# One row of the attention score by way of DRAM instead of two transposes, and a new order of work, in a four-layer graph network on one core

## The chip, the cores and the metric

The kernel runs on one core of a Trainium2 chip. The metric is the time of one execution on the device, in microseconds (us); smaller is better. The core's engines are named as the profile names them: PE (TensorE), DVE (VectorE), ACT (ScalarE), POOL (GpSimd) and SP (SyncE, which here only issues DMAs). Each runs its own instructions strictly in the order in which they are written, and waits on semaphores that the others raise.

## What is computed

32 graphs of 256 nodes with 256 features go through four layers. Each adds its output to its input and normalises over the features:

```python
x = _layernorm(x + _L0_gnn_ref(x, adj, W, b))      # ((adj @ (x @ W + b)) / row sums of adj
x = _layernorm(x + _L1_gnn_ref(x, adj, kernel))    # relu((adj @ x) @ kernel), masked
x = _layernorm(x + _L2_gnn_ref(x, adj, kernel, b)) # relu(D (adj + I) D x kernel + b)
x = _layernorm(x + _L3_gnn_ref(x, adj, Wv, bv, aw, ab, Wk, bk))
```

The last layer is the one that the change touches:

```python
sj = Xw @ aw[:d, 0]                      # Xw = X @ Wv + bv
si = Xw @ aw[d:, 0]
e = leaky_relu(sj[:, None, :] + si[:, :, None] + ab[0], negative_slope=0.2)
alpha_matrix = A * jnp.exp(e)
transition = alpha_matrix / (jnp.sum(alpha_matrix, axis=-1, keepdims=True) + 1e-12)
for k in range(3):
    H = H + Xk @ Wk[k] + bk[k]
    Xk = jnp.einsum('bij,bjd->bid', transition, Xk)
return relu(H)
```

So each graph needs its score once as a column (one number for each node, on the partitions) and once as a row of 256 numbers that every partition holds.

## The kernel before

The graphs are worked on four at a time: slot g = 0 to 3, group k = 0 to 7. A product is split into three fp32r parts (lo x hi, hi x lo, hi x hi) over two halves of the contraction and two output halves, which makes 12 matmuls. `product` (lines 262 to 264) and `product_by_turns` (line 272) write them. The "hi" part is a rounded copy, made on ACT (line 564), and the "lo" part is the rest, made on DVE or POOL.

The steps on PE are named s1 to s11, each for a slot and a group:

- s1: x W0; s2: adj times that, with the row sums in an extra column. Both are layer 0.
- s3, s4: layer 1. s5, s6: layer 2.
- s7: four transposes of x3, the input of layer 3 (line 341), so that `fea` holds it by features.
- s8a: x3 times Wk[0] and the two attention vectors. DVE adds the bias (`p0`, line 1261) into the tile P0, of which columns F and F+1 are the two scores of each node.
- s8b: x3 times Wk[1] and Wk[2], 512 columns wide, into the one PSUM tile `pair[1]`. ACT (`p12`) and DVE (`p2_lo`, line 1226) empty it.
- s9: two transposes of column F+1 of P0, broadcast over 128 columns (line 365). They leave the row of scores on all partitions in `ring[g]`.
- s10, s11: alpha times what came of s8b, and alpha times that (`q`, `q_hi`, `q_lo` between them).

After s9, ACT adds the column to the row (`logits`, line 624), DVE applies the leaky part (`leaky`), ACT takes exp (line 630), POOL multiplies by adj (`alpha`, line 959), and ACT and DVE split the result into `alpha_hi` and `alpha_lo`.

Each layer's normalisation runs DVE `statistics` (line 1206) and `variance_eps` (1211, 1212), POOL `power` and `mean_scale` (929, 946) and ACT `norm` (645). `norm(2, g, k)` writes X3, which also holds the output of layer 3, so it waits until the store of the group before (`x3_free`) is through.

The order of work on each engine is written out by hand in `first_iteration`, in `iteration(k)`, which a loop runs six times, and in `last_iterations`, which holds groups 6 and 7. Work of three groups is mixed in each: layers 2 and 3 of group k, layers 0 to 2 of group k+1, and s1 of group k+2. SP issues nearly all loads and stores in a fixed order of its own. Ahead of s1, PE runs 20 transposes on the identity matrix (`warm_up`, line 388).

Of the kernel before, what the change touches and what calls it, by code (L numbers as in the profile page):

```python
# [35 lines left out]
def build(nc, x, xT, adjT, w0, w1, w2, wk, wvT, aw, bv, ab, b0, b2, bk, out):  # L36
# [7 lines left out]
    with ExitStack() as ctx:  # L44
# [72 lines left out]
        y_ready = [sem4(f"y{l}_ready") for l in range(4)]  # L117
# [15 lines left out]
        P12_ready, Q_ready = sem("P12_ready"), sem("Q_ready")  # L133
        s_ready, e_ready, ex_ready, al_ready = sem("s_ready"), sem("e_ready"), sem("ex_ready"), sem("al_ready")
# [14 lines left out]
        def h_bank(g, first=False):  # L149
            return ring[g][:, :] if first else pair[g // 2][:, g % 2, :]  # L150

# [33 lines left out]
        def _(sp):  # L185
# [23 lines left out]
            def store(g, k):  # L209
                sp.wait_ge(x_ready[3][g], k + 1)  # L210
                sp.dma_start(graph(out, g, k), X3[g][:, :]).then_inc(x3_free[g], 16)

            def iteration(k, left):
# [13 lines left out]
                for g in range(SLOTS):  # L227
                    store(g, k)
# [26 lines left out]
        def _(pe):  # L255
# [68 lines left out]
            def s5(g, kn, first=False):  # L324
                pe.wait_ge(xd_lo_ready, count(g, kn))
                pe.wait_ge(diag_ready[g], kn + 1)
                if not first:
                    pe.wait_ge(y_ready[3][g], kn)
# [8 lines left out]
            def s7(g, k):  # L337
                pe.wait_ge(x_ready[2][g], k + 1)
                for f in range(2):
                    for t in range(2):  # L340
                        last = nc.tensor.transpose(ring[g][:, f * N + t * P:f * N + (t + 1) * P],  # L341
                                                   nodes(X3[g])[:, t, f * P:(f + 1) * P], ident[:, :])
                last.then_inc(s7_done[g], 1)
# [58 lines left out]
            def first_iteration():  # L402
                s1(0, 0, first=True)
                s2(0, 0, first=True)
                s1(1, 0, first=True)
                s1(2, 0, first=True)
                s1(3, 0, first=True)
                s2(1, 0, first=True)
                s2(2, 0, first=True)
                s2(3, 0, first=True)  # L410
                s1(0, 1, first=True)
                s3(0, 0, first=True)
                s3(1, 0, first=True)
                attention_vectors()
                s4(0, 0)
                s4(1, 0)
                s3(2, 0, first=True)
                s3(3, 0, first=True)
                s4(2, 0)
# [1320 lines left out]
```

## Time and profile before

| | |
|---|---|
| median of 3 runs | 560.35 us (559.84 to 560.39) |
| the profiled execution, its own time | 560.77 us |
| its span in the profile | 559.0 us |
| PE, busy | 536.1 us, 96% |
| DVE, busy | 499.7 us, 89% |
| POOL, busy | 459.1 us, 82% |
| ACT, busy | 418.5 us, 75% |
| data moved by DMA | 44.73 MB, mean 80 GB/s |

The span is what the profile covers, and the 1.8 us between it and the time of the same execution lie outside. Matmuls are pipelined: a matmul's own duration is longer than the distance between the starts of two, and the distance is what it costs.

### The profile page before, as it was taken

The page shows a single profiled execution, that of the slowest core. Times are in us where ns is not written, and L with a number is a line of the kernel's source. Part 1 is how long each engine was busy: PE and PEld are TensorE (multiplying, and loading weights), DVE is VectorE, ACT ScalarE, POOL GpSimd, SP SyncE. Part 2 cuts the span into 40 slices and gives each one's busy share as a digit, 9 for nine tenths or more (in the row PEclk, how much of TensorE's full clock was granted, in tenths as well). Part 3 has the DMA queues.
Part 4 walks back from the last instruction along what each step waited for, and adds up shares of the span by engine and source line. Part 5 has one row for each costly group of instructions (what it writes and reads, how often), then busy time and mean ns, then how long its engine had stood idle before and what let it go on. Part 6 is the DMA issues. An engine that isn't in the chain of part 4 may idle for free.

```text
span 559.0 us, 12279 instructions
## 1 busy us (share of the span) xinstructions
PE 536.1 (96%) x4064; PEld 511.6 (92%) x4064; DVE 499.7 (89%) x1221; ACT 418.5 (75%) x929; POOL 459.1 (82%) x575
## 2 busy tenths in 40 slices
PE   6799999999999999999999999999999999999983
PEld 6799999999999999999999999999999998998873
DVE  3999989989999889989899899998899898899676
ACT  4468787687876878687876978768796777875763
POOL 4688898989988899888989899888998898573253
PEclk9899999999999999999999999999999999999998
DMA  8824011340032301422114401324013300201001
GB/s 282 288 65 123 27 39 57 115 169 11 26 121 86 131 19 38 130 102 87 38 35 133 162 9 35 113 88 137 19 38 119 103 24 1 77 2 57 19 1 75
DMA packets 25222, 44.73 MB, mean 80 GB/s; under 512 B 3184, under 2 KB 3824, under 8 KB 25200
## 3 DMA queue, kind: packets, MB, share of 16 engines
q1 hardware_dynamic: 24336, 43.79, 24.3%
q10 hardware_dynamic: 864, 0.66, 0.4%
q8 instruction: 12, 0.20, 0.1%
q14 instruction: 10, 0.08, 0.0%
HBM read 36.05 MB, written 8.39 MB: 79 GB/s over the span
## 4 chain that ended last, share of the span: by engine, by line
PE 82%; DVE 10%; DMA 2%; issue 2%; ACT 2%; SPq 1%; POOL 0%; ACTq 0%; POOLq 0%; DVEq 0%
PE pair L272 37%; PE ring L262 12%; PE ring L264 12%; PE ring L263 12%; PE ring L341 3%; PE pair L262 2%; PE pair L264 2%; PE pair L263 2%; DVE stats L1206 2%; DMA xT_in<-xT_dram 1%; PE ring L365 1%; DVE ring L1286 1%; DVE nod_lo L1244 1%; DMA out_dram<-X 1%; DVE X L1235 1%
## 5 line engine op out<-in xcount | busy, mean ns | idle before, releaser
L645 ACT ACTIVATE X<-X,nmr,rstd 128x256 f32<-128x256 f32 x192 | 104.3, 596 | 51.6 <-POOL nmr L946 49.8
L929 POOL TENSOR_TENSOR rstd<-powin,minus_half 128x2 f32<-128x2 f32 (+1 forms) x124 | 104.1, 842 | 34.9 <-DVE nmean L1212 34.9
L1206 DVE BATCH_NORM_STATS2 stats<-X 128x6 f32<-128x512 f32 x128 | 89.9, 708 | 1.2
L262 PE MATMUL ring<-adj_hi,nod_lo 128*128 128x256 f32 x256 | 73.3, 286 | 1.3 <-DVE nod_lo L1244 1.3
L262 PE MATMUL ring<-W_hi,fea_lo 128*128 128x256 f32 x256 | 72.6, 284 | 1.0 <-DVE fea_lo L1198 1.0
L264 PE MATMUL ring<-adj_hi,nod_hi 128*128 128x256 f32 x256 | 72.3, 282 | 0.0
L263 PE MATMUL ring<-adj_lo,nod_hi 128*128 128x256 f32 x256 | 72.2, 282 | 0.0
L264 PE MATMUL ring<-W_hi,fea_hi 128*128 128x256 f32 x256 | 71.7, 280 | 0.0
L263 PE MATMUL ring<-W_lo,fea_hi 128*128 128x256 f32 x256 | 71.4, 279 | 0.0
L564 ACT ACTIVATE fea_hi<-ring 128x512 fp32r<-128x512 f32 x96 | 56.8, 593 | 18.4 <-PE ring L264 12.4
L1198 DVE TENSOR_TENSOR fea_lo<-ring,fea_hi 128x512 fp32r<-128x512 f32 x96 | 63.8, 683 | 6.5 <-ACT fea_hi L564 6.4
L959 POOL TENSOR_TENSOR tmp<-tmp,adj_in 128x512 f32<-128x512 f32 x32 | 46.7, 1467 | 23.4 <-ACT tmp L630 23.4
L262 PEld LDWEIGHTS ring<-adj_hi,nod_lo 128*128 128x128 f32 x256 | 48.7, 190 | 2.6 <-DVE nod_lo L1244 2.0
L262 PEld LDWEIGHTS ring<-W_hi,fea_lo 128*128 128x128 f32 x256 | 48.1, 188 | 1.7 <-issue 0.9
L263 PEld LDWEIGHTS ring<-adj_lo,nod_hi 128*128 128x128 f32 x256 | 48.8, 191 | 0.3
L264 PEld LDWEIGHTS ring<-adj_hi,nod_hi 128*128 128x128 f32 x256 | 48.8, 191 | 0.0
L263 PEld LDWEIGHTS ring<-W_lo,fea_hi 128*128 128x128 f32 x256 | 48.2, 188 | 0.0
L264 PEld LDWEIGHTS ring<-W_hi,fea_hi 128*128 128x128 f32 x256 | 48.1, 188 | 0.0
L917 POOL TENSOR_TENSOR adj_lo<-adj_in,adj_hi 128x512 fp32r<-128x512 f32 x32 | 41.0, 1299 | 8.3 <-ACT adj_hi L564 8.0
L967 POOL TENSOR_TENSOR h_lo<-P,h_hi 128x512 fp32r<-128x512 f32 x32 | 39.8, 1245 | 9.3 <-ACT h_hi L564 9.3
L952 POOL TENSOR_SCALAR X<-X,nmean,rstd 128x256 f32<-128x256 f32 x64 | 41.8, 662 | 1.1 <-POOL rstd L933 0.7
L272 PE MATMUL pair<-WB_hi,fea_lo 128*128 128x512 f32 x128 | 41.8, 407 | 0.2 <-DVE h_lo L1226 0.2
(123 smaller groups left out, 1910.0 us busy)
## 6 DMA issues: line engine op xcount, KB each, us to landing
adj_in<-adjT_dram SPq DMA_DIRECT2D x64, 256.0 KB, 2.8
xT_in<-xT_dram SPq DMA_DIRECT2D x32, 256.0 KB, 3.3
X<-x_dram SPq DMA_DIRECT2D x32, 256.0 KB, 2.6
out_dram<-X SPq DMA_DIRECT2D x32, 256.0 KB, 2.0
P<-wk_dram SPq DMA_DIRECT2D x3, 256.0 KB, 3.9
P<-w_dram SPq DMA_DIRECT2D x2, 256.0 KB, 5.9
X<-bk_dram SPq DMA_DIRECT2D x3, 128.0 KB, 4.2
P<-w_dram ACTq DMA_DIRECT2D x1, 256.0 KB, 3.8
```

What stands on the lines that cost most here:

```text
L262: mm(o, lhs(1, t, i), rhs(0, t), start=t == 0, stop=False)
L263: mm(o, lhs(0, t, i), rhs(1, t), start=False, stop=False)
L264: last = mm(o, lhs(0, t, i), rhs(0, t), start=False, stop=t == 1)
L272: last = mm(o, lhs(left, t, i), rhs(right, t), start=t == 0 and left == 1, stop=t == 1 and left == right)
L564: return nc.scalar.activation(dst, src, ACT.Copy)
L645: last = nc.scalar.activation(nodes(X[min(l + 1, 3)][g])[:, t, :], nodes(X[l][g])[:, t, :], ACT.Identity, scale=rstd[l][g][:, t:t + 1], bi ...
L917: tt(adj_lo[g][:, :], adj_in[g][:, :], adj_hi[g][:, :], ALU.subtract).then_inc(adj_ready, 1)
L929: tt(rstd[l][g][:, 0:n], powin[l][g][:, 0:n], minus_half[:, 0:n], ALU.pow).then_inc(rstd_ready[l], 1)
L952: last = ts(nodes(X1[g])[:, t, :], nodes(X0[g])[:, t, :], nmean[0][g][:, t:t + 1], rstd[0][g][:, t:t + 1], ALU.add, ALU.mult)
L959: tt(tmp[g][:, :], tmp[g][:, :], adj3_in[g][:, :], ALU.mult).then_inc(al_ready, 1)
L1198: tt(fea_lo[g][:, :], ring[g][:, :], fea_hi[g][:, :], ALU.subtract).then_inc(ready, 1)
L1206: nc.vector.bn_stats(stats[l][g][:, :], by_turns(X[l][g])).then_inc(st_ready[l], 1)
```

## The change

For groups 0 to 6, s9 goes. In its place SP waits for P0, stores its column F+1 to a small DRAM tensor (256 numbers, each 4 bytes), waits until that has landed, and loads it back as a row that is broadcast to all 128 partitions, into the second half of `tmp[g]`. `logits` waits for that load and reads `tmp` in place of the PSUM tile. Group 7 keeps s9.

With that, some waits change: s3 of the next group waits for `x3T_ready` and no longer for `s_ready`; s10 of an even slot waits for `p2_lo` of its own slot and not for that of slot 3; layers 2 and 3 count their `y_ready` on one semaphore each.

At the start, the loads of X0 come later (the first two slots' xT and adj first), and the loads of the attention vectors are issued by ACT only after the first h_hi parts. In group 7, x3 stands in X0 and not in X3, so `norm(2, g, 7)` doesn't wait for a store, and the last normalisation, that of slot 3, is done on DVE (`norm3`), with neither POOL's `mean_scale` nor ACT's `norm`. Finally the order of work is written anew on all engines, in all three parts.

```diff
+            def row_of_x3(g, k):
+                sp.wait_ge(P0_ready, count(g, k))
+                with nc.allow_non_contiguous_dma(reason="one number of each node"):
+                    sp.dma_start(row[g].rearrange("t p -> p t"), mixed(P0[g])[:, :, F + 1]).then_inc(row_out, 16)
+                sp.wait_ge(row_out, 16 * count(g, k))
+                sp.dma_start(nodes(tmp[g])[:, 1, :], row[g:g + 1].rearrange("a t p -> a (t p)").to_broadcast([P, N])).then_inc(row_in[g], 16)
...
-                if left >= 2:
+                if left >= 1:
+                    row_of_x3(0, k)
                     for g in range(SLOTS):
-                        load_x(g, k + 2)
-                if left >= 1:
+                        if g < SLOTS - 1:
+                            row_of_x3(g + 1, k)
+                        if left >= 2:
+                            load_x(g, k + 2)
                     for g in range(SLOTS):
                         load_adj3(g, k + 1)
...
             for g in range(SLOTS):
-                for load in (load_xT, load_adj, load_x):
+                for load in (load_xT, load_adj):
                     load(g, 0, before=False)
+                if g >= 1:
+                    load_x(g - 1, 0, before=False)
+            load_x(SLOTS - 1, 0, before=False)
...
             def s3(g, kn, first=False):
                 pe.wait_ge(x1_lo_ready, count(g, kn))
                 if not first:
-                    pe.wait_ge(s_ready, count(g, kn - 1))
+                    pe.wait_ge(x3T_ready, count(g, kn - 1))
...
                 pe.wait_ge(al_lo_ready, count(g, k))
-                pe.wait_ge(P2_ready, count(SLOTS - 1, k))
+                pe.wait_ge(P2_ready, count(SLOTS - 1 if g % 2 else g, k))
...
             def first_iteration():
                 s1(0, 0, first=True)
+                s1(1, 0, first=True)
                 s2(0, 0, first=True)
-                s1(1, 0, first=True)
+                s2(1, 0, first=True)
                 s1(2, 0, first=True)
                 s1(3, 0, first=True)
-                s2(1, 0, first=True)
                 s2(2, 0, first=True)
                 s2(3, 0, first=True)
-                s1(0, 1, first=True)
                 s3(0, 0, first=True)
...
-                s9(0, k)
+                s3(0, k + 1)
+                s7(2, k)
                 s8a(1, k)
-                s7(2, k)
-                s3(0, k + 1)
                 s8b(1, k)
+                s7(3, k)
                 s8a(2, k)
                 s4(0, k + 1)
-                s9(1, k)
-                s9(2, k)
-                s7(3, k)
+                s8a(3, k)
                 s8b(2, k)
...
-            def logits(g, k):
-                act.wait_ge(s9_done, count(g, k))
+            def logits(g, k, last=False):
+                if last:
+                    act.wait_ge(s9_done, g + 1)
+                else:
+                    act.wait_ge(row_in[g], 16 * k + 16)
+                summand = ring[g][:, 0:N] if last else nodes(tmp[g])[:, 1, :]
...
-            def norm(l, g, k):
+            def norm(l, g, k, last=False):
                 act.wait_ge(nmr_ready[l], count(g, k))
-                if l == 2:
+                if l == 2 and not last:
                     act.wait_ge(x3_free[g], 16 * k + 16)
...
+            def norm3(g, k):
+                dve.wait_ge(rstd_ready[3], count(g, k))
+                for t in range(2):
+                    half = X0[g][:, t * F:(t + 1) * F]
+                    last = ts(half, half, nmean[3][g][:, t:t + 1], rstd[3][g][:, t:t + 1], ALU.add, ALU.mult)
+                last.then_inc(x_ready[3][g], 1)
```

How the change moves instructions is seen at three places.

The first is SP, inside its loop, behind the four loads of xT. Before, the four loads of X0 and the loads of adj for layer 3 follow:

```order
L192 DMA xT_in<-xT_dram 128x512
L197 DMA X_0<-x_dram 128x512
L197 DMA X_1<-x_dram 128x512
L197 DMA X_2<-x_dram 128x512
L197 DMA X_3<-x_dram 128x512
```

Now (register instructions of the waits stand between):

```order
L216 DMA row_dram<-P_1 128x2x1
L217 REGISTER_ALU
L218 DMA tmp<-row_dram 128x256
L201 DMA X_0<-x_dram 128x512
L214 REGISTER_ALU
L216 DMA row_dram<-P_2 128x2x1
L217 REGISTER_ALU
L218 DMA tmp<-row_dram 128x256
L201 DMA X_1<-x_dram 128x512
```

Each row is a store and a load, and SP waits for the first before it issues the second; the loads of X0 stand between the rows.

The second is DVE at the start, from the first xT_lo on. L1295 is `first_xT_lo`, L1202 `h_lo_part`, L1217 and L1218 `sums0`, L1308 `first_x_bias`, L1302 `first_y0`. Before:

```order
L1295 TENSOR_TENSOR xT_lo0<-xT_in0,xT_hi0 128x512
L1202 TENSOR_TENSOR h_lo0<-ring0,h_hi0 128x2x256
L1295 TENSOR_TENSOR xT_lo1<-xT_in1,xT_hi1 128x512
L1295 TENSOR_TENSOR xT_lo2<-xT_in2,xT_hi2 128x512
L1295 TENSOR_TENSOR xT_lo3<-xT_in3,xT_hi3 128x512
L1217 TENSOR_SCALAR powin0_0<-pair0 128x2
L1218 RECIPROCAL rinv0<-pair0 128x2
L1202 TENSOR_TENSOR h_lo1<-ring1,h_hi1 128x2x256
L1202 TENSOR_TENSOR h_lo2<-ring2,h_hi2 128x2x256
L1202 TENSOR_TENSOR h_lo3<-ring3,h_hi3 128x2x256
L1308 TENSOR_TENSOR X0_0<-X0_0,b0_bc 128x512
```

Now, where L1323, L1336, L1217, L1237, L1238 and L1330 are the same functions:

```order
L1323 TENSOR_TENSOR xT_lo1<-xT_in1,xT_hi1 128x512
L1336 TENSOR_TENSOR X0_0<-X0_0,b0_bc 128x512
L1217 TENSOR_TENSOR h_lo0<-ring0,h_hi0 128x2x256
L1323 TENSOR_TENSOR xT_lo2<-xT_in2,xT_hi2 128x512
L1217 TENSOR_TENSOR h_lo1<-ring1,h_hi1 128x2x256
L1237 TENSOR_SCALAR powin0_0<-pair0 128x2
L1238 RECIPROCAL rinv0<-pair0 128x2
L1330 SCALAR_TENSOR_TENSOR X0_0<-pair0,rinv0,X0_0 128x256 x2
L1224 BN_STATS stats0_0<-X0_0 128x6
```

The part for slot 3's xT and the h_lo parts of slots 2 and 3 have moved behind `first_y0` of slot 0.

The third is the end of DVE's program. Before, it closes with slot 3's variance and mean:

```order
L1286 SCALAR_TENSOR_TENSOR ring3<-ring3,rinv3,P0_3 128x256 x2
L1211 TENSOR_SCALAR powin3_2<-stats3_2 128x2
L1212 TENSOR_SCALAR nmean3_2<-stats3_2 128x2
L1291 SCALAR_TENSOR_TENSOR X3_3<-ring3,X3_3 128x512
L1206 BN_STATS stats3_3<-X3_3 128x6
L1211 TENSOR_SCALAR powin3_3<-stats3_3 128x2
L1212 TENSOR_SCALAR nmean3_3<-stats3_3 128x2
```

Now:

```order
L1312 SCALAR_TENSOR_TENSOR X0_3<-ring3,X0_3 128x512
L1224 BN_STATS stats3_3<-X0_3 128x6
L1231 TENSOR_SCALAR powin3_3<-stats3_3 128x2
L1232 TENSOR_SCALAR nmean3_3<-stats3_3 128x2
L1318 TENSOR_SCALAR X0_3<-X0_3,nmean3_3,rstd3_3 128x256 x2
```

The order of the rest is as it was; two instructions of 128x256 have been added behind it.

## Rows read from the trace of the kernel before

**Rows 1.** The page: an engine's busy time, and the clock in 40 slices.

```profile
PE 536.1 (96%) x4064; PEld 511.6 (92%) x4064; DVE 499.7 (89%) x1221; ACT 418.5 (75%) x929; POOL 459.1 (82%) x575
PEclk9899999999999999999999999999999999999998
```

**Rows 2.** Busy time by stretch: stretch, its length, each engine's busy us, PEclk, DMA.

```profile
123.83:189.27 65.44, 65.44 (x507) 63.04 (x506) 60.83 (x149) 51.70 (x116) 59.00 (x73) 1.00 0.25 80
```

**Rows 3.** What PE waited for in the whole span: us in total, times, longest.

```profile
PE pair L272 <- DVE X L1302: 3.1, 1, 3.1
PE pair L272 <- issue: 1.7, 1, 1.7
PE pair L272 <- DVE h_lo L1202: 1.4, 1, 1.4
PE ring L262 <- DVE nod_lo L1244: 1.3, 2, 0.9
PE ring L341 <- ACT X L645: 1.0, 1, 1.0
```

**Rows 4.** Timeline of PE around an s7 and an s9: start, us, instruction.

```profile
462.19 0.60 PE L341 MATMUL ring<-ident,X 128*128 128x128 f32 x4
462.63 0.38 PE L365 MATMUL ring<-ident,P 128*128 128x128 f32 x2
462.76 0.48 PE L272 MATMUL pair<-WA_hi,fea_lo 128*128 128x258 f32 x2
463.09 0.40 PE L272 MATMUL pair<-WA_lo,fea_hi 128*128 128x258 f32 x2
```

**Rows 5.** Timeline of PE at the start: the first matmul of s1(0), and two successive ones.

```profile
6.62 0.36 PE L262 MATMUL ring<-W_hi,xT_lo 128*128 128x256 f32 x1 [1.34 <-DVE xT_lo L1295]
...
11.87 0.28 PE L264 MATMUL ring<-W_hi,xT_hi 128*128 128x256 f32 x1
11.99 0.28 PE L262 MATMUL ring<-W_hi,xT_lo 128*128 128x256 f32 x1
```

**Rows 6.** The chain that ended last, 0 to 60 us: start, us, what.

```profile
5.12 8.17 DMA xT_in<-xT_dram
...
19.96 0.88 DVE X L1302 x2
...
30.56 0.79 PE pair L396 x8
...
49.60 0.39 PE ring L262
```

**Rows 7.** Busy time by stretch, after the long wait at the start.

```profile
21.00:23.00 2.00, 2.00 (x11) 2.00 (x12) 1.82 (x8) 0.00 (x0) 0.81 (x2) 0.60 1.04 260
```

**Rows 8.** DMA issues, KB each, us to landing: 0 to 40 us.

```profile
ab_bc<-ab_dram ACTq DMA_DIRECT2D x1, 0.5 KB, 6.6
```

**Rows 9.** The same, in the whole span.

```profile
adj_in<-adjT_dram SPq DMA_DIRECT2D x64, 256.0 KB, 2.8
out_dram<-X SPq DMA_DIRECT2D x32, 256.0 KB, 2.0
```

**Rows 10.** Timeline of ACT in a group of the loop: start, us, instruction.

```profile
210.56 0.60 ACT L564 ACTIVATE fea_hi<-ring 128x512 fp32r<-128x512 f32 x1
211.04 0.85 ACT L624 ACTIVATE tmp<-ring,P 128x256 f32<-128x256 f32 x2
```

**Rows 11.** The chain that ended last: an s8b of group 0.

```profile
66.71 2.81 PE pair L272 x12
```

**Rows 12.** The chain that ended last, 500 to 559 us.

```profile
512.43 4.09 DMA out_dram<-X
...
516.61 1.10 ACT X L645 x2
...
554.36 0.70 POOL rstd L929
...
555.36 0.60 ACT X L645
```

More of the change, by code:

```diff
@@ L731, in iteration @@
                 from_ring(2, s7_done, k, fea_hi, x3T_hi_ready)
-                xT_hi_part(1, k + 2)
                 from_ring(0, s3_done, k + 1, fea_hi, t1_hi_ready)
                 norm(2, 3, k)
+                logits(0, k)
+                from_ring(3, s7_done, k, fea_hi, x3T_hi_ready)
+                xT_hi_part(3, k + 2)
+                x1_hi(1, k + 1)
+                p12(1, k)
+                x1_sum(1, k + 1)
+                x1_hi(2, k + 1)
+                logits(1, k)
+                exp(0, k)
@@ new lines, in iteration @@
+                p12(2, k)
+                exp(1, k)
+                diag_hi(0, k + 1)
+                x1_hi(3, k + 1)
+                from_ring(1, s3_done, k + 1, fea_hi, t1_hi_ready)
+                alpha_hi_part(0, k)
+                logits(2, k)
+                logits(3, k)
+                from_ring(2, s3_done, k + 1, fea_hi, t1_hi_ready)
+                exp(2, k)
+                exp(3, k)
+                p12(3, k)
+                alpha_hi_part(1, k)
+                x1_sum(2, k + 1)
@@ new lines, in last_iterations @@
+            def last_iterations(k):
+                h_hi_part(0, k + 1)
+                adj_hi_part(0, k + 1)
+                h_hi_part(1, k + 1)
+                h_hi_part(2, k + 1)
+                h_hi_part(3, k + 1)
+                adj_hi_part(1, k + 1)
+                adj_hi_part(2, k + 1)
+                adj_hi_part(3, k + 1)
+                z0(0, k + 1)
+                z0(1, k + 1)
+                norm(2, 0, k)
+                norm(2, 1, k)
+                from_ring(0, s7_done, k, fea_hi, x3T_hi_ready)
+                z0(2, k + 1)
+                z0(3, k + 1)
+                from_ring(1, s7_done, k, fea_hi, x3T_hi_ready)
+                norm(2, 2, k)
+                p12(0, k)
+                x1_hi(0, k + 1)
+                from_ring(2, s7_done, k, fea_hi, x3T_hi_ready)
+                norm(2, 3, k)
+                logits(0, k)
@@ new lines, in last_iterations @@
+                norm(2, 0, k + 1, last=True)
+                from_ring(2, s5_done, k + 1, fea_hi, t2_hi_ready)
+                from_ring(0, s7_done, k + 1, fea_hi, x3T_hi_ready)
+                from_ring(3, s5_done, k + 1, fea_hi, t2_hi_ready)
+                norm(2, 1, k + 1, last=True)
+                from_ring(1, s7_done, k + 1, fea_hi, x3T_hi_ready)
+                norm(2, 2, k + 1, last=True)
+                p12(0, k + 1)
+                logits(0, k + 1, last=True)
+                from_ring(2, s7_done, k + 1, fea_hi, x3T_hi_ready)
@@ L867, in last_iterations @@
+                norm(2, 3, k + 1, last=True)
+                p12(1, k + 1)
+                logits(1, k + 1, last=True)
+                from_ring(3, s7_done, k + 1, fea_hi, x3T_hi_ready)
+                norm(3, 0, k)
                 exp(0, k + 1)
-                p12(1, k + 1)
-                norm(2, 3, k + 1)
-                logits(1, k + 1)
-                from_ring(3, s7_done, k + 1, fea_hi, x3T_hi_ready)
+                exp(1, k + 1)
                 p12(2, k + 1)
-                exp(1, k + 1)
@@ L1390, in first_iteration @@
                 xd_lo(1, 0)
-                weights_lo()
                 xd_lo(2, 0)
```

961 lines of the change are left out of this document (457 added, 504 removed).

## Prediction

> **What bounds the kernel now.** I read the page first: PE is busy 96% of the span, and its clock is at the full 2.4 GHz but for the second and the last of 40 slices [rows 1]. Then the stretches: one turn of the loop (group 1's, the others differ by some hundredths) takes 65.44 us, and PE is busy for 65.44 of them, while DVE has 60.83, POOL 59.00 and ACT 51.70 [rows 2]. So the loop, six turns and 393 us of the span, is PE's own work without a hole, and what leaves PE there leaves the time. Then the waits: all that PE waits for in the whole span lies outside the loop [rows 3], the longest 3.1 and 1.4 us at the start and 1.7 and 1.0 us in the last two groups. Last, the chain to the first 60 us, and the chain of the end [rows 6, 12].
>
> **What s9 costs.** One place shows it: s7's four transposes start at 462.19, s9's two at 462.63, the next matmul pair at 462.76, and that pair then takes 0.33 us to the next where pairs otherwise follow in 0.24 [rows 4]. s7 takes 0.44 and leaves the same 0.09 behind it when it stands alone; together they cost 0.57 + 0.09 = 0.66, of which I give s9 a third, 0.22 us. The change takes 28 of the 32 away: 28 x 0.22 = **6.1 us**, 0.88 in each turn of the loop. The bounds: 28 x 0.13 = 3.6 us if the slower pair behind is not saved, 6.2 at most.
>
> **What comes in its place.** Two DMAs a graph, on SP's queue, which PE never waits for. Neither has its like in the trace. The store is 256 numbers of 4 bytes; nearest are the 256 KB store of the output, 2.0 us, and the 4-byte broadcast of ab in the crowded start, 6.6 us [rows 8, 9]. The load is 1 KB into each partition; nearest are the 256 KB loads, 2.8 us, and again 6.6 [rows 9, 8]. A quarter of the DMA engines' time is taken in the loop [rows 2], so I take values near the uncrowded rows: 2.8 for the store, 2.5 for the load, and with two issues of about 0.45 on SP some 6.2 us for a row.
>
> The Trainium skill (DMA: Bandwidth & Descriptors, rules for kernel authors, and the anatomy of one DMA) says that a strided last dimension becomes one descriptor for each element, and that a DMA has about 2 us that don't depend on its size, most of it the receipt of the write. By that, two dependent DMAs are an estimated 4 us before any descriptor; the trace's 2.0 us for an output store agrees with the second rule, and no row here shows the first.
>
> Is there room for 6.2 us? I lay the new order of PE on a line, with s6(0) at 0, 1.43 us for a product of twelve 256-column matmuls (steps of 0.12 [rows 5]), 0.44 for s7, 2.81 for s8b [rows 11]. s8a(0) ends at 13.8, and s10(0), the first to need alpha, comes at 36.0 (before, at 39.7). Slot 0's row is back at about 21, and ACT reaches `logits(0)` at 20 and has nothing urgent until s7(3) ends at 23.2. Slots 2 and 3 are closer: P0(2) is ready at about 26, SP issues its store, waits, issues the load, a load of X0, then slot 3's store, waits again: 26 + 2 x (0.45 + 2.8) + 3 x 0.45 - 0.45 + 2.5, about 36. ACT wants it at 35 to 36, by steps of about 0.5 us per instruction [rows 10]. What is queued behind `logits(3)` on ACT is from_ring(2), exp(2), exp(3), p12(3) and alpha_hi(1); PE's s10(1), at 41.8, needs the last, split on DVE. With slot 3's row at 36 alpha_hi(1) is through at about 40.7 and DVE, in its own order, comes to the split just ahead of 42; until the row is some 0.8 us later still, it costs PE nothing. Slot 2's q must pass DVE, ACT and POOL by s11(2) at 51.8, and I find it there at 52.0. So nothing is far late, and some of it has no slack: DVE's 60.8 us now stand in a turn of 64.57, 94%, and POOL's 59.0, 91%. I charge **1.0 us** for small holes over all turns; between 0 (as now) and 5 us (0.7 a turn, nearly all of what s9 gave).
>
> **The start.** s1(0) begins at 6.62 us [rows 5]; s5(2) begins at 49.60 [rows 6], and with it and s5(3), 2.9 us, s6(0) begins at 52.5. Between lie 24 products and the attention vectors' 12 small matmuls (8 of them in 0.79 [rows 6], so 1.2), 24 x 1.43 + 1.2 = 35.5 us of work in 45.9 us, so 10.4 are lost. Why: DVE holds its part of xT_in[3] (landed at 13.3, after 8.17 us) ahead of `first_y0(0)` at 19.96, which frees the PSUM pair for s2(2) [rows 6]; PE waits 3.1 us for it [rows 3], and then runs at a granted clock of 0.60 [rows 7], between 1.2 and 2.4 GHz: 11 matmuls in 2.00 us, 0.18 each for 0.12, so about 1.5 us more over the 24 of two s2.
>
> Now s1(1) fills the 1.4 us hole ahead of s2(0) (its xT is one load earlier). Then h_hi(1) on ACT waits behind xT_hi(2), which lands at about 10.1 by my estimate (the tenth load lands at 13.3, at 0.8 us a load, and it is now the sixth): s2(1) starts at 12.1, a hole of 0.9. `first_y0(0)` is through at 13.2, seven us earlier, so s2(2) and s2(3) wait only for their h_lo parts on DVE, about 0.7 each. s3(0) waits about 2.0 for x1_lo(0), which stands behind x_bias and y0 of slots 2 and 3. Behind it the products follow one another until s5(0), which waits 1.1 for xd_lo(0), behind `weights_lo` (some seven full-tile steps, about 4 us if a half tile takes 0.44 [rows 6] and a full one 0.6). These holes are my count along the new order, 5.4 us in all, with 0.4 for the slower first matmuls behind them: s6(0) at about 6.6 + 35.5 + 5.8 = 47.9. That is **4.5 us** less. Bounds: a gain of only 1.5 us if the 2 us hole also brings the low clock and DVE has another as long; of 8 us if the holes close.
>
> **The end.** From 500 us on PE idles in the waits of [rows 3]. The 1.0 us for ACT is `norm(2, 1)`, which waits for the store of the group before, 4.09 us in the chain [rows 12]; with x3 in X0 that wait is gone. The other holes there are at most 1.3, some of them for nod_lo on DVE [rows 3]. The 1.7 us ahead of s10(0) is p12(3) and p2_lo(3) after the last s8b; s10(0) no longer waits for them, but s10(1) does, 0.5 us after it could start. Counting on from there, DVE gets q(0) done at +3.3 and not +5.1 us, s11(0) starts at +5.4 and not +7.1, and then DVE's own chain of q, z3, y3 and statistics, which is full in both, brings most of it back: the last mean is 0.7 us earlier. `norm3` then costs two DVE instructions of 128x256 where POOL's product, two hand-overs and ACT's two instructions took from 554.36 + 0.70 = 555.06 to 555.36 + 1.10 = 556.46 [rows 12]. Such instructions on DVE take 0.44 each in other rows (first_y0's two, 0.88 [rows 6]); 0.9 for 1.4 saves 0.5. Sum: 1.0 + 0.5 (of the 1.3) + 0.7 + 0.5 = **2.7 us**. Bounds 0 (the holes move) and 5 (all close).
>
> **Sum.** 560.77 (the profiled execution's own time) - 6.1 - 4.5 - 2.7 + 1.0 = 548.5 us. That execution lay 0.42 above the median of the runs, so 548.1 us on the median's scale, 2.2% under it.
>
> **The rivals.**
>
> First, *the rows come late, and it ends slower than before*. The place is `logits(2)` and `logits(3)` on ACT, behind which stand exp, p12 and alpha_hi. My count has slot 3's row at 36 and 0.8 us of slack behind it. If each DMA takes X, it is back at 27.8 + 3 X, since SP waits for slot 2's store first. It decides where seven groups lose 13.3 us, 1.9 each: 27.8 + 3 X = 36.7 + 1.9, X = 3.6 us. At X = 4 a group loses 3.1, and the kernel takes 560.35 + 21.7 - 13.3 = 569 us; at 6.6, ab's in the crowd, far over 600. For it speaks that every element is a piece of its own; against it that the loop's DMA is mostly idle, and that uncrowded transfers a thousand times larger land in 2.0 to 2.8. Chance 0.08; about 569.
>
> Second, *another engine sets the turn*. DVE's 60.8 and its hand-overs don't shrink, and with PE's order tighter the turn stays near 65.3. Then the start, the end and 7 x 0.15 us count: 560.35 - 4.5 - 2.7 - 1.1 = 552 us. For it: 94% on DVE, and two places where I found needs and supplies within 0.3 us. Against it: in the trace before, equally close orders left PE no hole in 65.44 us. Chance 0.16.
>
> Third, *the start gives nothing*: holes of 2 us bring the granted clock of 0.60, as one of 3.1 us did while two of 1.4 didn't. Then 1.5 us in place of 4.5: 551 us. Chance 0.10, and the range holds it.
>
> Fourth, *all holes close* at start, end and in the loop: 560.35 - 6.1 - 8 - 4 = 542 us. Chance 0.06.
>
> **Chances and range.** The forecast has 0.60. The range, 543.5 to 555, holds the forecast, the second and the third, and leaves out the first and most of the fourth and of a wider second. Differences under 0.2% (1.1 us) can't be told from none in this kernel. Faster by more than that: all but the first rival and a piece of the second, 0.91; within 0.2%, 0.02; slower, 0.07.
>
> **What would show it.** In the profile after, PE has 56 fewer transposes, and its busy time is about 6 us less. The turn of the loop is about 64.6 us with PE busy throughout; if it is 65.4, the second rival is right, and the engine that PE waits for says where. If ACT's `tmp` of `logits` waits long for a DMA of `row_dram`, it is the first. s6(0) starts at about 48 us; the granted clock at 15 to 30 us tells the third. In the chain of the end, DVE's `norm3` takes under 1 us. I am wrong if a row takes much over 6 us to return, if the holes at the start don't shrink, or if PE's own work has grown at a place that I took as moved only.

## The result, and the profile after

The changed kernel takes 763.23 us (median of 4 runs, 760.77 to 766.86) against 560.37 us of the kernel before in the same job (4 runs, 559.84 to 561.73). The ratio is 1.361, interval 1.358 to 1.365: **slower by 203 us**. The forecast was 548.1 us. The profiled execution took 760.91 us, with a span of 759.1.

The page of the changed kernel: busy time of each engine, the granted clock, the shares of the chain that ended last, and one DMA row (size, median us to landing):

```profile
PE 580.8 (77%) x4008; PEld 540.8 (71%) x4008; DVE 518.7 (68%) x1223; ACT 415.3 (55%) x927; POOL 444.8 (59%) x574
...
PEclk9999877998779987799887997879988799779999
...
DMA 40%; DVE 37%; PE 11%; issue 6%; ACT 3%; SPq 2%; POOL 1%; ACTq 0%; DVEq 0%; POOLq 0%
...
row_dram<-P SPq DMA_DIRECT2D x28, 1.0 KB, 9.6
```

PE had 96% [rows 1] and has 77%. Its busy time has grown by 45 us although 56 transposes are gone, and the granted clock falls from 2.4 to 1.2 GHz twice in each turn. In the second turn it is 0.50 from 176.4 to 183.2 us and from 200.3 to 217.4, the second time with PE idle since 196.7 us; each matmul takes longer in these stretches. In the kernel before it fell once, at the start [rows 7]. The chain that ended last is a DMA's for 40% of the span. The last row is the price that the forecast had at 2.8 us: the row's store lands after 9.6 us.

The waits of the changed kernel over the span (engine and line, what it waited for, us in total, times, longest):

```profile
POOL tmp L975 <- ACT tmp L642: 200.9, 18, 18.5
ACT tmp L637 <- DMA tmp<-row_dram: 198.3, 27, 12.1
DVE tmp L1285 <- ACT tmp L637: 137.9, 21, 10.7
...
PE ring L279 <- DVE fea_lo L1213: 76.6, 7, 13.7
```

L637 is `logits`, L1285 the leaky part, L975 `alpha`: the wait for the row is handed down through ACT, DVE and POOL. PE's longest wait isn't for alpha. It is for `fea_lo` of layer 1, a step with no need of the row. It stands on DVE behind the leaky part, and its `fea_hi` on ACT behind `logits`, and those need the row.

SP's queue in the second turn (start, us, line, transfer; L216 is the row's store, L218 its load back, L201 a load of X0), from the store of slot 1's row on:

```profile
171.70 0.37 SPq L216 DMA_DIRECT2D row_dram<-P  x1
181.15 0.32 SPq L218 DMA_DIRECT2D tmp<-row_dram  x1
181.58 0.37 SPq L201 DMA_DIRECT2D X<-x_dram  x1
182.06 0.37 SPq L216 DMA_DIRECT2D row_dram<-P  x1
```

And the chain through it, with the first store of the next turn:

```profile
163.21 8.03 DMA row_dram<-P
171.70 9.44 DMA row_dram<-P
182.06 10.42 DMA row_dram<-P
193.44 9.51 DMA row_dram<-P
202.96 4.91 DMA tmp<-row_dram
258.26 8.04 DMA row_dram<-P
```

Four stores stand end to end, since SP waits for each to land before it issues anything else: 8.03 + 9.44 + 10.42 + 9.51 = 37.4 us, then a load of 4.9, and 2.3 for what SP issues between them, 44.7 us from P0(0) to the last row. A turn is 258.26 - 163.21 = 95.05 us, against 65.44 [rows 2].

### The profile page after: what moved, and what is told of

Same layout as the page of the kernel before. It is cut to its first block, busy times and chain, and to the rows that moved or that the text cites. A ratio compares the mean times of both kernels' runs of the same rounds, so it can differ in the third digit from the quotient of the medians.

```text
span 759.1 us, 12235 instructions
## 1 busy us (share of the span) xinstructions
PE 580.8 (77%) x4008; PEld 540.8 (71%) x4008; DVE 518.7 (68%) x1223; ACT 415.3 (55%) x927; POOL 444.8 (59%) x574
## 4 chain that ended last, share of the span: by engine, by line
DMA 40%; DVE 37%; PE 11%; issue 6%; ACT 3%; SPq 2%; POOL 1%; ACTq 0%; DVEq 0%; POOLq 0%
DMA row_dram<-P 33%; DVE stats L1224 6%; PE pair L289 6%; DMA tmp<-row_dram 5%; DVE nod_lo L1264 4%; DVE ring L1306 3%; DVE ring L1272 3%; DVE P L1298 3%; DVE powin L1231 3%; DVE h_lo L1217 2%; DVE X L1312 2%; DVE nmean L1232 2%; DVE X L1255 2%; PE ring L279 1%; DVE X L1277 1%
## 5 line engine op out<-in xcount | busy, mean ns | idle before, releaser
L975 POOL TENSOR_TENSOR tmp<-tmp,adj_in 128x512 f32<-128x512 f32 x32 | 41.6, 1305 | 201.4 <-ACT tmp L642 200.9
L279 PE MATMUL ring<-W_hi,fea_lo 128*128 128x256 f32 x256 | 75.9, 297 | 76.6 <-DVE fea_lo L1213 76.6
L637 ACT ACTIVATE tmp<-tmp,P 128x256 f32<-128x256 f32 x56 | 25.4, 501 | 198.3 <-DMA tmp<-row_dram 198.3
L945 POOL TENSOR_TENSOR rstd<-powin,minus_half 128x2 f32<-128x2 f32 (+1 forms) x124 | 99.8, 806 | 57.3 <-DVE nmean L1232 57.2
L1285 DVE SCALAR_TENSOR_TENSOR tmp<-tmp 128x512 f32<-128x512 f32 x32 | 22.0, 689 | 138.0 <-ACT tmp L637 137.9
L281 PE MATMUL ring<-W_hi,fea_hi 128*128 128x256 f32 x256 | 75.0, 293 | 0.0
L289 PE MATMUL pair<-WB_hi,fea_lo 128*128 128x512 f32 x128 | 45.9, 442 | 15.0 <-DVE h_lo L1246 15.0
L289 PE MATMUL pair<-WA_hi,fea_lo 128*128 128x258 f32 x128 | 31.4, 330 | 33.5 <-DVE P L1281 33.5
L280 PEld LDWEIGHTS ring<-W_lo,fea_hi 128*128 128x128 f32 x256 | 51.6, 202 | 0.0
L281 PEld LDWEIGHTS ring<-W_hi,fea_hi 128*128 128x128 f32 x256 | 51.5, 201 | 0.0
```

What stands on the lines that cost most here:

```text
L279: mm(o, lhs(1, t, i), rhs(0, t), start=t == 0, stop=False)
L280: mm(o, lhs(0, t, i), rhs(1, t), start=False, stop=False)
L281: last = mm(o, lhs(0, t, i), rhs(0, t), start=False, stop=t == 1)
L289: last = mm(o, lhs(left, t, i), rhs(right, t), start=t == 0 and left == 1, stop=t == 1 and left == right)
L945: tt(rstd[l][g][:, 0:n], powin[l][g][:, 0:n], minus_half[:, 0:n], ALU.pow).then_inc(rstd_ready[l], 1)
L975: tt(tmp[g][:, :], tmp[g][:, :], adj3_in[g][:, :], ALU.mult).then_inc(al_ready, 1)
```

## The experiments

Three theories stood behind them. **A**: the rows' latency, in series on SP, is the loss. **B**: the new order is. **C**: leaving s9 out never gave 6 us, since another chain sets the turn. Later ones are named where they come in. Each kernel was timed beside the kernel before.

### Without the rows, and the rows alone

```diff
-                    row_of_x3(0, k)
-                            row_of_x3(g + 1, k)
...
-                    act.wait_ge(row_in[g], 16 * k + 16)
-                summand = ring[g][:, 0:N] if last else nodes(tmp[g])[:, 1, :]
+                    act.wait_ge(P0_ready, count(g, k))
+                summand = ring[g][:, 0:N] if last else bk_bc[:, 0:N]
```

> The changed kernel with both DMAs of the row left out in groups 0 to 6: logits adds the bias tile bk_bc in place of the row, so the output is not the reference's. Theory A (the two DMAs of a row, 9.6 and 4.6 us to landing and issued one after another by SP, make all the loss): the turn of the loop falls from 95.3 to about 65 us, PE is busy all through it, and the time is 548 to 553 us (the start gained 1.3 us and not 4.5). Theory B (the new order and the new waits lose by themselves): the turn stays well over 66 us and the time is over 565 us.

577.17 us against 561.27, ratio 1.0275 (1.0217 to 1.0332). So 186 of the 203 us are the rows, and some 16 us are the new order's own. Theory A missed its 548 to 553 us, and what theory B named did happen (a turn of 68.67 us, over 565 us in all): both are right in part, and A has by far the larger part. The second kernel is the kernel before with nothing but the rows in place of s9:

> The kernel before, with the row by DRAM in groups 0 to 6 in place of the transposes, and nothing else of the change but the two waits that it needs. Theory A: SP's chain of four rows, some 45 us, is the loss in any order; the turn is 90 to 105 us and the time 720 to 800 us, much like the changed kernel. Theory B: the old order keeps most of its time, under 650 us.

```diff
+                    row_of_x3(0, k)
...
-                s9(0, k)
...
-                act.wait_ge(s9_done, count(g, k))
+                    act.wait_ge(row_in[g], 16 * k + 16)
```

825.22 us, ratio 1.471 (1.466 to 1.476), over the 800 that theory A had at most. The rows alone cost 264 us in the old order, and not by SP's series alone. In the chain of its second turn stand three rows, each with its load (8.65 + 4.87, 8.69 + 4.40 and 8.74 + 4.95 us), and between them steps of ACT, DVE and PE: P0 of the next slot is made behind work that waits for the row of another. The new order bears the rows better and still isn't made for them.

In the kernel without rows the room that a row has can be read. DVE's P0 of the four slots in one turn:

```profile
206.07 0.69 DVE L1278 TENSOR_TENSOR P<-pair,bk_bc 128x516 f32<-128x516 f32 x1
212.88 0.69 DVE L1278 TENSOR_TENSOR P<-pair,bk_bc 128x516 f32<-128x516 f32 x1
215.69 0.69 DVE L1278 TENSOR_TENSOR P<-pair,bk_bc 128x516 f32<-128x516 f32 x1
220.79 0.68 DVE L1278 TENSOR_TENSOR P<-pair,bk_bc 128x516 f32<-128x516 f32 x1
```

And ACT's logits of the same slots, the last row with slots 2 and 3 (slot 3's half of it from 225.5 on):

```profile
211.90 0.91 ACT L634 ACTIVATE tmp<-bk_bc,P 128x256 f32<-128x256 f32 x2
219.03 0.90 ACT L634 ACTIVATE tmp<-bk_bc,P 128x256 f32<-128x256 f32 x2
...
224.67 1.71 ACT L634 ACTIVATE tmp<-bk_bc,P 128x256 f32<-128x256 f32 x4
```

From the end of P0 to the logits there are 5.1, 5.5, 8.3 and 4.0 us, and 18.8 from the first P0 to the last logits. The changed kernel needs 44.7 for the same stretch: 25.9 us more. Its turn is 95.05 - 68.67 = 26.4 us longer than this kernel's. The rows' loss is that stretch, once for each of the seven groups (7 x 26.4 = 185 us).

### What sets the store's price

The kernel before, with four small stores more in each turn whose landing nothing waits for but their own next issue; slot 0's has the changed kernel's form:

```diff
+                    sp.dma_start(dst, src).then_inc(side_done[g], 16)
...
+            forms = [(side["fa"].rearrange("t p -> p t"), b2_bc[:, :].rearrange("p (t f) -> p t f", t=2)[:, :, 5]),
+                     (side["fb"], b2_bc[:, 0:2]),
+                     (side["fc"], b2_bc[:, 0:1]),
+                     (side["fd"][:, :, 0].rearrange("t p -> p t"), b2_bc[:, :].rearrange("p (t f) -> p t f", t=2)[:, :, 5])]
```

fa is 256 numbers of 4 bytes side by side in DRAM, as the row is; fb 128 pieces of 8 bytes side by side; fc 128 numbers of 4 bytes side by side; fd 256 numbers of 4 bytes, one every 64 bytes.

> The kernel before, with four small stores more in each turn of the loop that nothing waits for: 256 numbers of 4 bytes side by side in DRAM (as the row's), 128 pieces of 8 bytes, 128 pieces of 4 bytes, and 256 of 4 bytes that lie 64 bytes apart. Theory C (the price goes by the number of pieces): 8 to 10 us for both forms of 256, 4.5 to 6 for both of 128. Theory D (it goes by pieces that meet in the same lines of DRAM): side by side 8 to 10, 64 bytes apart 3 to 4; 128 of 8 bytes about 5 to 8. The kernel's own time stays within 1 us of before in both.

```profile
fa_dram<-b_bc SPq DMA_DIRECT2D x6, 1.0 KB, 9.8
fb_dram<-b_bc SPq DMA_DIRECT2D x6, 1.0 KB, 8.3
fc_dram<-b_bc SPq DMA_DIRECT2D x6, 0.5 KB, 10.2
fd_dram<-b_bc SPq DMA_DIRECT2D x6, 1.0 KB, 5.9
```

These are the page's DMA rows: count, size, median us to landing. The time is 561.63 us (one run), so the stores cost the kernel nothing where nobody waits. Half as many pieces (fc) cost as much as all (fa): it isn't their number. But the four rows can't be compared as they stand. fb is issued while fa is still landing, and fd while fc is:

```profile
X<-x_dram SPq DMA_DIRECT2D x1, 256.0 KB, 7.5
...
211.50:214.00 2.50, 2.50 (x12) 2.01 (x12) 2.50 (x7) 2.50 (x7) 2.50 (x4) 1.00 0.00 0
```

The first line is a load of X0 that SP issued at 210.96 us, just before fb (211.40) and 6 us behind fa (204.99, landed at 214.69). In the kernel before such a load takes 2.5 us. The second has the columns of [rows 2]: for 2.5 us no DMA engine does anything, though the load and fb are both waiting. At the same place of the next kernel, where the store ahead is 1 KB in one piece, the load takes 2.6 us and the engines are busy for 0.43 of the stretch. So a store of pieces side by side holds back what is issued behind it until it has landed. fb waited 3.0 to 3.7 us for fa in this way, and fd 3.0 to 3.4 for fc. Without that wait an estimate is 5.0 us for fb and 2.8 for fd (medians of six).

A second kernel took four other forms:

> The same, with four other stores: 1 KB from one partition in one piece, 128 pieces of 64 bytes, 256 of 4 bytes with a node's two numbers side by side (as neighbours 4 bytes apart), and 256 of 4 bytes that lie 512 bytes apart. Theory C: about 2.5, 4.5 to 6, 8 to 10 and 8 to 10 us. Theory D: about 2.5, 2.5 to 4, 8 to 10, and 3 to 4 us.

```profile
fh_dram<-b_bc SPq DMA_DIRECT2D x6, 8.0 KB, 2.4
...
fi_dram<-b_bc SPq DMA_DIRECT2D x6, 1.0 KB, 5.7
```

fh is 128 pieces of 64 bytes, fi 256 numbers 512 bytes apart. Eight times the bytes land in 2.4 us. fi stands behind fg, whose form is side by side, and the load of X0 issued just ahead of fi takes 6.0 to 6.9 us, so fi's 5.7 hold such a wait as well. Theory D fits all of this: numbers of 4 bytes side by side make 10 us, 8-byte pieces side by side some 5, and numbers 64 bytes apart hardly more than whole 64-byte pieces. It isn't shown that a line of 64 bytes is the limit, since nothing between 8 and 64 bytes of distance was tried. The landing of the 1 KB store from one partition (ff) and of fg isn't shown by the profile.

### The changed kernel with a quick store

```diff
-                    sp.dma_start(row[g].rearrange("t p -> p t"), mixed(P0[g])[:, :, F + 1]).then_inc(row_out, 16)
+                    sp.dma_start(row[:, :], b2_bc[:, 0:16]).then_inc(row_out, 16)
...
-                sp.dma_start(nodes(tmp[g])[:, 1, :], row[g:g + 1].rearrange("a t p -> a (t p)").to_broadcast([P, N])).then_inc(row_in[g], 16)
+                sp.dma_start(nodes(tmp[g])[:, 1, :], b2.to_broadcast([P, N])).then_inc(row_in[g], 16)
```

> The changed kernel with both DMAs of a row in their places, but with other data: the store writes 64 bytes from each of 128 partitions (2.4 us in a run of mine) in place of 256 numbers of 4 bytes (7.9 to 10.4 us), the load spreads 1 KB of b2 to the partitions as before (4.6 us). The logits' row is then b2 and not the graph's own. A row takes about 2.4 + 4.6 + 1.0 = 8 us in place of 15. Theory A (the landing of the scattered store is what costs, through SP's wait, four times in a turn): between 7 and 28 us a turn come back of the 26.6 that the rows cost: turn 69 to 77 us, time 577 to 635 us. Rival (two dependent DMAs on SP cost it whatever the store's form, by taking the queue from the other loads): turn over 85, time over 700 us.

580.92 us, ratio 1.035 (1.033 to 1.038).

```profile
tmp<-b_dram SPq DMA_DIRECT2D x28, 128.0 KB, 3.1
...
row_dram<-b_bc SPq DMA_DIRECT2D x28, 8.0 KB, 1.4
```

Both DMAs, both waits and the order of SP's queue are as in the changed kernel, and of the rows' 32% over the kernel without them all but 0.8%, some 4 us, is gone. A row takes 1.4 + 3.1 us, about 4.5 (the landing is counted from the issue), within the 4 to 8 us that there are. This is what shows A: with the same DMAs, waits and order, the rows cost some 4 us at 4.5 us a row and 186 at 9.6 + 4.6. It doesn't tell the store from the load, since both are quicker here.

### One latency a row, and none in SP's series

```diff
-                sp.wait_ge(row_out, 16 * count(g, k))
-                sp.dma_start(nodes(tmp[g])[:, 1, :], ...).then_inc(row_in[g], 16)
```

The store itself now signals `row_in`.

> The changed kernel with the row's store alone: SP doesn't wait for it, there is no load, and ACT's logits wait for the store to land and add the bias tile (the logits' row isn't the graph's own; the load's work is left out). So each row costs one latency of 8 to 10.4 us, and none waits behind another's. Without rows, logits(g) comes 5.1, 5.5, 8.3 and 4.0 us behind its P0, so the stores are 2 to 6 us late. Theory A (latency, in series on SP): turn 69 to 75 us, time 580 to 620 us, against 763 with both DMAs in series. Rival J (the store's latency alone is the loss, the series and the load matter little): over 700 us.

653.9 us, ratio 1.167 (1.159 to 1.174): between the two expectations, and neither had the reason. The chain of this kernel in its second turn:

```profile
155.35 9.74 DMA row_dram<-P
...
165.12 0.92 ACT tmp L635 x2
...
166.06 0.69 DVE tmp L1283
166.75 0.62 DVE P L1279
...
167.39 13.00 DMA row_dram<-P
```

SP doesn't put these two stores in series; DVE does. P0(3), which the last store waits for, stands on DVE behind the leaky part of slot 1, which waits for that slot's store. So two latencies (here 9.7 and 13.0) stand end to end in each turn whatever SP does. The 13.0 is longer than a store alone; it was issued 4.8 us behind slot 2's. That was in the order of the instructions, and I hadn't looked for it: a late row delays the next one's making.

### What s9's absence is worth

The kernel before without s9 in groups 0 to 6, no rows, nothing moved:

```diff
-                s9(0, k)
...
-                s9(3, k)
...
-                act.wait_ge(s9_done, count(g, k))
+                    act.wait_ge(P0_ready, count(g, k))
```

> The kernel before, with s9 left out in groups 0 to 6 and no row in its place: logits adds the bias tile, so the output is not the reference's; s3 waits for x3T_ready. All else, the order too, is as before. If the term of 6.1 us is right, the turn of the loop is 64.6 us and the time 554 to 555. It also tells theory A from theory B for the run without rows (577 us, turn 68.7): if the old order keeps PE full at 64.6, then the new order of the loop itself costs 4.1 us a turn; if the old order's turn also stays at 65.4 or more, something that comes with the missing s9 does.

560.32 us against 559.96, ratio 1.0003 (0.9988 to 1.0018): nothing. The stretch of one turn, columns as in [rows 2]:

```profile
189.20:254.60 65.40, 65.16 (x498) 62.43 (x497) 60.03 (x149) 51.52 (x116) 59.17 (x73) 1.00 0.25 78
```

PE's own 65.44 have become at most 65.16, and the turn is 65.4 to 65.5 as before. Along the turn PE is 0.69 us early at s4(1) (36.18 us behind s6(0), where the kernel before has 36.87), 0.46 at s10(0), and no longer early at s4(3) (48.36 in both). The holes are short: s10(0) starts 1.72 us behind s4(2), where the kernel before has 1.40, and s4(3) 1.66 behind s11(0) for 1.42. s4(3) needs `fea_lo` of slot 3, which DVE makes behind the attention steps. So one product was put ahead of it:

```diff
-                s4(3, k + 1)
                 s1(0, k + 2)
+                s4(3, k + 1)
```

> The kernel before without s9 in the loop (the summand of the logits is the bias tile; work left out), as in the run before it of that kind, and with one product's place changed: s1(0, k+2) stands ahead of s4(3, k+1) on PE and not behind it. In the run without s9 PE was 0.69 us early at s4(1) and no longer early at s4(3): s4(3) waits for fea_lo of slot 3, at the end of a chain through DVE. Theory C (a chain of other engines, hidden under PE, has the same 65.5 us turn): the hole ahead of s4(3) closes, since PE has s1(0) to do there, but the chain itself isn't shorter, so that the turn stays at 65.2 to 65.6 us, or grows if s4(3) is now late by a whole product; time 558 to 561 us. Rival F (only the one place in PE's order eats the gain): the turn goes to 64.7 to 65.0, time 555 to 557 us.

561.54 us, ratio 1.0014 (0.9998 to 1.003). The long step of the chain that opens a turn, of two turns:

```profile
126.76 5.99 PE pair L272 x48
192.23 5.99 PE pair L272 x48
```

The turn is 65.47, and the rival, that one place in PE's order ate the gain, falls. C's forecast holds. Its reason, a chain over the other engines that is as long as PE's work was, and hidden since PE never waited for it, fits the holes, but no run shortened that chain, and which steps make it is open.

### Why the new order is slow without the rows

Without the rows the turn is 68.67 us, columns as above:

```profile
198.43:267.10 68.67, 66.35 (x497) 62.42 (x497) 63.47 (x149) 51.57 (x117) 58.25 (x73) 1.00 0.23 76
```

DVE has grown from 60.83 to 63.47 us with the same 149 instructions. Four kinds of step that read only SBUF are longer: the two `nod_lo` and the small ones of variance and mean (0.28 for 0.19 us). Two others with both sources in SBUF are shorter: the leaky part takes 0.68 us for 1.05, and `alpha_lo` 0.68 for 0.82. The statistics (L1221, 0.71) and those that read PSUM (`fea_lo`, 0.68) are unchanged. DVE at one place of it:

```profile
252.65 2.70 DVE L1261 SCALAR_TENSOR_TENSOR nod_lo<-X,rstd,nod_hi 128x256 fp32r<-128x256 f32 x4
```

and POOL beside it (L926 is `x_bias`, the addition of b0 to X0):

```profile
253.53 1.54 POOL L926 TENSOR_TENSOR X<-X,b_bc 128x512 f32<-128x512 f32 x1
```

Four such steps take 1.66 us where POOL does something else. The test cuts x_bias to 4 columns:

```diff
-                tt(nodes(X0[g]), nodes(X0[g]), b0_bc[:, :].unsqueeze(1).to_broadcast([P, 2, F]), ALU.add).then_inc(xb_ready, 1)
+                tt(nodes(X0[g])[:, :, 0:2], nodes(X0[g])[:, :, 0:2], b0_bc[:, 0:2].unsqueeze(1).to_broadcast([P, 2, 2]), ALU.add).then_inc(xb_ready, 1)
```

> The changed kernel without the row DMAs (logits add the bias tile), and POOL's x_bias, a step of 1.5 us for each graph that reads two tiles in SBUF, cut to 4 of its 256 columns (b0 isn't added; work left out). Without the rows alone: 577.2 us, a turn of 68.7 us, DVE's nod_lo (xd_lo) 0.61 us on average where the kernel before has 0.51, powin 0.28 where it has 0.19. Theory G (in the new order DVE's steps that read SBUF lie beside POOL's more often, and are stretched while POOL works): nod_lo falls toward 0.51 to 0.56, and the turn by 0.5 to 3 us, to 65.7 to 68.2; time 558 to 574 us. Rival H (the stretching doesn't matter, or doesn't come from POOL): turn and nod_lo as in the run without rows, 576 to 578 us.

571.48 us, ratio 1.0198 (1.0181 to 1.0215). DVE's two kinds of `nod_lo` without the rows, 198 to 268 us (count, busy, mean ns):

```profile
L1261 DVE SCALAR_TENSOR_TENSOR nod_lo<-X,rstd,nod_hi 128x256 fp32r<-128x256 f32 x8 | 4.5, 606 | 0.0
L1256 DVE TENSOR_TENSOR nod_lo<-X,nod_hi 128x512 fp32r<-128x512 f32 x4 | 4.1, 1034 | 0.4 <-ACT nod_hi L570 0.4
```

and with the bias cut as well:

```profile
L1256 DVE TENSOR_TENSOR nod_lo<-X,nod_hi 128x512 fp32r<-128x512 f32 x4 | 4.2, 1039 | 0.4 <-ACT nod_hi L570 0.4
L1261 DVE SCALAR_TENSOR_TENSOR nod_lo<-X,rstd,nod_hi 128x256 fp32r<-128x256 f32 x8 | 3.7, 511 | 0.0
```

L1261 falls to the 0.51 us that it has in the kernel before, L1256 stays. The turns begin at 194.96, 262.81 and 330.65 us, 67.85 apart, 0.8 less. So POOL's bias beside `nod_lo` is shown to cost 0.8 of the 3.2 us that the new order's turn is longer. The other 2.4 aren't taken apart. What the trace shows is that PE now waits for DVE, POOL and ACT at five places in each turn, none over 0.9 us, about 2.3 us in all, and that the second half of the turn's chain is DVE's.

### The start and the end alone

The kernel before with the new start (the order of `first_iteration` on all engines and the loads), with the new end (X0 for group 7, and `norm3`), and with both, each with s9 and the old order in the loop:

```diff
+                s1(1, 0, first=True)
                 s2(0, 0, first=True)
+                s2(1, 0, first=True)
...
-            def norm(l, g, k):
+            def norm(l, g, k, last=False):
...
-                if l == 2:
+                if l == 2 and not last:
```

> The kernel before with the new first part alone: the loads of the start and all engines' first_iteration. By the changed kernel's trace s6(0) then starts at 51.2 us and not at 52.5: 559.0 us, 1.3 less. By my prediction's term it would be 555.9. If the old loop takes up work that the new start leaves behind, within 0.5 us of before.

> The kernel before with two things of the end alone, in the old order: group 7's x3 in X0, without the wait for the store, and slot 3's last normalisation on DVE. By my terms 1.0 + 0.5 us: 558.9. If what follows norm(2, 1) is bound by the copies between the s8b of the slots and not by its start, only the 0.5 us: 559.9.

> Both of these together on the kernel before, with s9 in all groups and the old order of the loop: the sum of the two, 557.5 us if both terms hold as last put (1.3 and 1.5), 559 if only the smaller ones do. It should be faster than before and than the changed kernel.

| | us | before, same job | ratio |
|---|---|---|---|
| new start | 558.32 | 559.96 | 0.9976 (0.9955 to 0.9998) |
| new end | 558.84 | 559.96 | 0.9975 (0.9962 to 0.9988) |
| both | 557.60 | 559.96 | 0.9967 (0.9944 to 0.9989) |

Both intervals lie under 1, that of the start only just. With both, the median is the lowest of this study, 0.3% under the kernel before, and 557.60 is what the sum of the two terms had (557.5). `norm3` on DVE at the end, against [rows 12]:

```profile
551.17 0.73 DVE L1309 TENSOR_SCALAR X<-X,nmean,rstd 128x256 f32<-128x256 f32 x2 [0.81 <-POOL rstd L939]
```

## Why the prediction was wrong

- **The row's price** was the step that failed. "I take values near the uncrowded rows: 2.8 for the store, 2.5 for the load" should have read 9.6 and 4.6. (The two issues of 0.45 should not have been added, since the landing is counted from the issue.) I chose the nearest row by how crowded the stretch is and by how many bytes move. The ab broadcast, also in pieces of 4 bytes and at 6.6 us [rows 8], was the nearest in form, and even that was too little. Crowding isn't what makes it: in the uncrowded loop of an otherwise unchanged kernel the same form takes 9.8 us.
- **The first rival** was what happened, at a chance of 0.08. Its place, `logits` on ACT, is right. Its limit holds as far as tried: with 1.4 and 3.1 us a transfer, under its 3.6, the rows cost almost nothing. "Far over 600" at 6.6 us was the right direction, though the formula gives 623 there. The formula, 27.8 + 3 X, was too kind: by it the last row would be at 27.8 + 9.6 + 9.6 + 4.6 = 51.6, 15 us late, and the time about 651. It starts at P0(2) as if SP were free then. At 9.6 us a store SP is still busy with the rows of slots 0 and 1, and four stores stand in the sum, not two. The chance was too small: the form of the pieces was named for this rival and then outweighed by bytes and quiet.
- **"What leaves PE leaves the time", 6.1 us** for s9, was wrong as well, and so were its bounds of 3.6 to 6.2: with nothing else changed, s9's absence gave nothing. On PE it was worth 0.69 us a turn, which the other engines' steps took back. The second rival had the mechanism ("another engine sets the turn"), and its 65.3 us is close to the measured 65.5. A PE busy for all of 65.44 us [rows 2] says that PE has no slack; it doesn't say that the others have.
- **The line of PE's new order** put needs and supplies within 0.3 us of each other and charged 1.0 us for all turns. The new order costs 3.2 us a turn without the rows, 16 us in all (six turns make 19, of which the start and the end give some back). Failed: "in the trace before, equally close orders left PE no hole". Durations on DVE were carried over from the old order, and 0.8 us of the 3.2 is shown to come from DVE steps that lengthen beside POOL. The rest is open.
- **The start**, 4.5 us forecast: s6(0) begins at 51.17 in the changed kernel, for 52.58 before, 1.4 less, and the new start alone gives 1.6 us by the medians (0.1 to 2.5 by the interval). Two things failed. The work between was put at 35.5 us, and PE's busy time says 37.8 (6.82 to 51.17 us), so fewer of the 45.9 us were holes than I thought. And the holes did not shrink: PE idles 6.4 us of that stretch before and 6.6 after. PE's waits in the first 60 us:

```profile
PE pair L289 <- DVE h_lo L1217: 1.8, 3, 0.8
PE ring L279 <- DVE xT_lo L1323: 1.6, 2, 0.9
PE ring L279 <- DVE nod_lo L1259: 1.6, 1, 1.6
...
PE ring L279 <- DVE nod_lo L1264: 1.5, 1, 1.5
PE pair L413 <- DMA ab_bc<-ab_dram: 0.8, 1, 0.8
```

  7.3 us in these five rows, 0.85 of it ahead of s1(0). The second wait for xT_lo and that for ab (whose load is issued later now) weren't in my count at all.

- **The third rival**, the low clock at the start, is not settled by the changed kernel's page, which has none there. It comes and goes with either order. The same 3.4 us of the new start alone, and of both:

```profile
28.70:32.10 3.40, 3.40 (x18) 3.40 (x18) 1.59 (x6) 1.33 (x4) 3.40 (x5) 0.50 0.87 331
...
28.70:32.10 3.40, 3.40 (x31) 3.40 (x30) 2.17 (x6) 2.48 (x7) 3.40 (x5) 1.00 0.91 344
```

  PE gets 18 matmuls started in the one and 31 in the other, and s6(0) begins at 52.06 and 50.51 us. With the old start it begins at 52.58 where the clock fell (the kernel before) and at 52.15 and 52.20 where it didn't (without s9; with the new end). So the new start gives 1.0 to 1.7 us where neither has the low clock, and little or nothing where it has. That the changed kernel's profiled execution had none was luck.
- **The end**, 2.7 us forecast: the run of the new end holds only two of its four terms, 1.0 for the store's wait and 0.5 for `norm3`, and gives 1.1 by the medians (0.7 to 2.1 by the interval). In the profiled executions it is 2.4 (from the last group's first long step to the end of the span, 104.3 us before, 101.9 with the new end). `norm3`'s two halves are through 0.75 us after POOL's last `power`, where ACT's took 1.40 [rows 12] and the forecast had 0.9. These two terms stand; the other 1.2 us, from the new order of the last group, were not run alone.

## What to carry to other kernels

A transfer on a dependent path is priced by its form first: look in the trace for a row with pieces of the same size, and let it weigh more than one with the same bytes or in the same quiet stretch. Here pieces of 4 bytes side by side made most of the difference between 4.5 and 14 us a row, and a queue that waits for each landing made it count four times. Before a term "what leaves the busiest engine leaves the time" is written down, follow one item through all the engines over a turn: at 93% on a second engine, the turn can be that engine's chain already. When the price of a transfer is measured by a trial, nothing slow may stand ahead of it in the queue, or its landing holds the other's wait. And where the changed order lets a late result stand ahead of the step that makes the next one (leaky(1) ahead of P0(3)), a latency counts twice, whatever the queue does.

## What the hardware showed that I had not expected

- A store into DRAM of 4-byte pieces side by side lands after 9.8 us (256 of them) or 10.2 (128 of them), and 128 pieces of 64 bytes after 2.4, or 1.4 where nothing is issued just ahead of them. Numbers 64 bytes apart take 5.9, of which 3.0 to 3.4 are the wait for the store ahead, and 8-byte pieces side by side 8.3, with 3.0 to 3.7 of such a wait. The Trainium skill (DMA: Bandwidth & Descriptors, Specifications) says that below 512 B the DMA engine does a read-modify-write. That fits pieces side by side that wait for one another, which no run here shows; the 64-byte pieces, under 512 as well, show no such price. The same page (Anatomy of one DMA) has a fixed cost of about 2 us, for DMAs that GpSimd issues. These are SP's: the 64-byte pieces agree with it, and the pieces side by side don't.
- Such a store holds back the transfers issued behind it: a 256 KB load takes 6.0 to 7.5 us behind one, for 2.4 to 2.8 in the kernel before, and the DMA engines stand idle meanwhile.
- The broadcast of 1 KB to 128 partitions takes 4.6 us behind a store of the same bytes, and 3.1 from a tensor that nothing writes. Why is open.
- The low clock at the start comes in some executions of an order and not in others. With the new start s6(0) begins at 52.06 us in an execution that has it, and at 50.51 in one that hasn't.
- `nod_lo` on DVE, with two sources in SBUF, lengthens beside a POOL step that reads SBUF: by 0.1 us in 0.51 on average and up to 1.0 in 1.66 for four, and it is back at 0.51 with the POOL step cut. `fea_lo`, with a source in PSUM, stays at 0.68. The Trainium skill (Advanced Engine Details and Errata, GPSIMD Details) says that POOL shares a read and a write interface with DVE, and conflicts with DVE instructions in a 2-port mode or with two SBUF inputs. This case agrees.
